# A decoder layer on one core: exponentials moved between ScalarE, VectorE and GpSimd

## The reference, cut to what matters

```python
# recurrence, for each feature, k = block input, v = ctx, ed = exp(-w), eg = exp(w)
out = A + jnp.exp(u + kk) * (vv * Bm + jnp.maximum(t - 1.0, 0.0))
A = ed * A + inc * jnp.exp(kk) * vv
Bm = eg * Bm + inc * jnp.exp(-kk)
# gates
logits = jnp.einsum('bsh,eh->bse', x, Wg)
Sm = jnp.swapaxes(jax.nn.softmax(logits, axis=-1), 1, 2)
```

## Time and profile before

| | |
|---|---|
| median of 3 runs | 1078.71 us (1078.17 to 1080.0) |
| profiled execution | 1075.21 us, of which its span is 1073.5 us |
| PE busy | 961.7 us (90%) |
| DVE busy | 738.1 us (69%) |
| ACT busy | 695.5 us (65%) |
| POOL busy | 103.8 us (10%) |
| mean granted clock of TensorE | 0.961 |

### The profile page before, as it was taken

One profiled execution on the slowest core, in us unless ns is written; L12 is line 12 of the kernel. 1 busy time (PEld: TensorE's weight loads), 2 busy tenths in 40 slices (PEclk: granted clock), 3 DMA queues, 4 the chain that ended last, 5 costly groups with the idle time before them and its releaser, 6 DMA issues.

```text
span 1073.5 us, 19089 instructions
## 1 busy us (share of the span) xinstructions
PE 961.7 (90%) x7280; PEld 868.4 (81%) x7280; DVE 738.1 (69%) x1476; ACT 695.5 (65%) x1231; POOL 103.8 (10%) x115
## 2 busy tenths in 40 slices
PE   6557788989799989999899989999899998999997
PEld 5457687778688878888798878988798887989997
DVE  6657758675687667776777748786667757555665
ACT  6347676666557766666676757566676666756775
POOL 2012001200130011200111001200012001000000
PEclk9669889999899999999999999999999999999999
DMA  6013233222122222222222222222222222232350
GB/s 197 28 53 97 81 108 116 62 59 70 60 80 70 70 70 88 59 80 83 75 81 77 64 87 79 60 80 60 79 80 79 60 70 77 82 118 89 101 186 11
DMA packets 89242, 86.49 MB, mean 81 GB/s; under 512 B 5944, under 2 KB 89152, under 8 KB 89152
## 3 DMA queue, kind: packets, MB, share of 16 engines
q1 hardware_dynamic: 89152, 85.27, 26.0%
HBM read 83.15 MB, written 2.10 MB: 79 GB/s over the span
## 4 chain that ended last, share of the span: by engine, by line
PE 70%; DVE 16%; ACT 10%; issue 3%; DMA 0%; POOL 0%; SPq 0%; POOLq 0%; ACTq 0%; DVEq 0%
PE up_ps L403 10%; PE up_ps L405 9%; PE up_ps L404 9%; PE down_ps L611 9%; PE down_ps L613 9%; PE down_ps L612 8%; DVE w_lo L786 4%; PE bank L403 3%; PE bank L404 3%; PE bank L405 3%; DVE h_lo L786 2%; ACT L670 2%; PE bank L454 2%; ACT w_hi L735 1%; ACT probs L670 1%
## 5 line engine op out<-in xcount | busy, mean ns | idle before, releaser
L724 ACT ACTIVATE h_all<-up_ps,b_all 128x512 f32<-128x512 f32 (+1 forms) x296 | 182.2, 630 | 299.1 <-PE up_ps L405 297.1
L611 PE MATMUL down_ps<-w_hi,h_hi 128*128 128x256 f32 x1024 | 297.9, 291 | 40.5 <-DVE h_lo L786 40.5
L786 DVE TENSOR_TENSOR w_lo<-w_raw,w_hi 128x512 fp32r<-128x512 f32 x296 | 206.8, 712 | 165.2 <-ACT w_hi L735 164.9
L613 PE MATMUL down_ps<-w_hi,h_lo 128*128 128x256 f32 x1024 | 291.8, 285 | 0.0
L612 PE MATMUL down_ps<-w_lo,h_hi 128*128 128x256 f32 x1024 | 291.7, 285 | 0.0
L611 PEld LDWEIGHTS down_ps<-w_hi,h_hi 128*128 128x128 f32 x1024 | 197.6, 193 | 52.0 <-DVE w_lo L786 39.6
L403 PE MATMUL up_ps<-x2t_hi,w_hi 128*128 128x512 f32 (+1 forms) x592 | 224.3, 379 | 0.0
L404 PE MATMUL up_ps<-x2t_lo,w_hi 128*128 128x512 f32 (+1 forms) x592 | 218.8, 370 | 0.0
L405 PE MATMUL up_ps<-x2t_hi,w_lo 128*128 128x512 f32 (+1 forms) x592 | 218.6, 369 | 0.0
L612 PEld LDWEIGHTS down_ps<-w_lo,h_hi 128*128 128x128 f32 x1024 | 197.9, 193 | 5.1
L613 PEld LDWEIGHTS down_ps<-w_hi,h_lo 128*128 128x128 f32 x1024 | 197.8, 193 | 0.0
(11 more groups left out here) (174 smaller groups left out, 1347.4 us busy)
## 6 DMA issues: line engine op xcount, KB each, us to landing
w_raw<-in_w_dram SPq DMA_DIRECT2D x296, 256.0 KB, 2.8
x_in<-in_x_dram SPq DMA_DIRECT2D x8, 256.0 KB, 3.2
ctx_sb<-in_ctx_dram SPq DMA_DIRECT2D x8, 256.0 KB, 3.1
out_dram<-acc SPq DMA_DIRECT2D x8, 256.0 KB, 3.2
w_raw<-in_wq_dram SPq DMA_DIRECT2D x1, 256.0 KB, 3.0
w_raw<-in_wk_dram SPq DMA_DIRECT2D x1, 256.0 KB, 4.1
w_raw<-in_wv_dram SPq DMA_DIRECT2D x1, 256.0 KB, 4.2
w_raw<-in_wo_dram SPq DMA_DIRECT2D x1, 256.0 KB, 4.6
```

Of the source, the lines that this page charges most:

```text
L611: nc.tensor.matmul(ps, hi, w2h[:, c, :], start=c == 0 and j == 0, stop=False, skip_group_check=True)
L613: mm = nc.tensor.matmul(ps, lo, w2h[:, c, :], start=False, stop=c == FC - 1 and j == PAIR - 1, skip_group_check=True)
L724: a = nc.scalar.activation(h_all[:, unit % HALL, k * wide:(k + 1) * wide], up_ps[unit % 2][:, k * wide:(k + 1) * wide], ACT.Gelu_apprx_tan ...
L786: return nc.vector.tensor_tensor(dst, src, hi.bitcast(F32), ALU.subtract)
```

## The change

The two `exp_uk` instructions on ACT are gone. A small tile `exp_u` = exp(u) is computed once in the setup, and the product on DVE becomes, in two halves, (`mix` * `exp_u`) * `exp_k`. Since `exp_k` is now needed there, `mix` lies in the tile `exp_uk`. The routing exponential goes from ACT to POOL, as e to the power of `logits`, with a constant tile `euler` full of e. In POOL's list it stands at step 62 of the pair's train.

```diff
-        mix = exp_k[:]
+        mix = exp_uk[:]
...
                     nc.scalar.activation(exp_k[:], k, ACT.Exp)
-                    for c in range(C):
-                        nc.scalar.activation(exp_uk[:, c], k[:, c], ACT.Exp, bias=wu[:, 1, c:c + 1])
...
-                if part == 3:
-                    act.wait_ge(route_step, 4 * b + 2)
-                    nc.scalar.activation(route_exps[:], logits[:], ACT.Exp).then_inc(route_exp, 1)
...
                 if s == V_STEP:
+                    nc.scalar.activation(exp_u[:], wu[:, 1, :], ACT.Exp)
...
                     dve.wait_ge(xa_step, 6 * p + 5)
-                    nc.vector.tensor_tensor(mix, mix, exp_uk[:], ALU.mult).then_inc(xa_step, 1)
+                    for c in range(C):
+                        i = nc.vector.scalar_tensor_tensor(out=mix[:, c], in0=mix[:, c], scalar=exp_u[:, c:c + 1], in1=exp_k[:, c],
+                                                           op0=ALU.mult, op1=ALU.mult)
+                    i.then_inc(xa_step, 1)
...
+            def route(b):
+
+                pool.wait_ge(route_step, 4 * b + 2)
+                nc.gpsimd.tensor_tensor(route_exps[:], euler[:], logits[:], ALU.pow).then_inc(route_exp, 1)
...
+            nc.gpsimd.memset(euler[:], math.e)
...
             for s in FIRST_ORDER[1:]:
                 attend(0, s)
+                if s == ROUTE_STEP[3]:
+                    route(0)
...
                         if p < NPAIR:
                             attend(p, s)
+                            if s == ROUTE_STEP[3]:
+                                route(p)
```

More of the change, by code:

```diff
@@ L3 @@
 import itertools
+import math
 from contextlib import ExitStack
@@ L100, in decoder_layer @@
         decay = sb("decay", [P, 2, C])
+        exp_u = sb("exp_u", [P, C])
         decay_row = sb("decay_row", [P, 2, C, S])
@@ L110, in decoder_layer @@
         eps_row = sb("eps_row", [P, PAIR])
+        euler = sb("euler", [P, PAIR, E])
         x_in = sb("x_in", [P, PAIR, D])
```

## The result

| | before | after |
|---|---|---|
| median of 5 runs each | 1078.71 us (1075.67 to 1080.0) | 1086.67 us (1084.75 to 1087.7) |
| profiled execution (its span) | 1075.21 us (1073.5) | 1087.0 us (1085.3) |
| mean granted clock in it | 0.961 | 0.956 |

The ratio is 1.0073, with a 95% interval of 1.0060 to 1.0086: the change makes the kernel slower by 8.0 us in the medians. The two profiled executions lie 11.8 us apart, because the one of before is among its fastest.

The account below looks back on a forecast made before the run. TensorE, busy 90%, was taken to bound the kernel. Terms -5.0 - 1.1 + 1.6 - 0.5 + 12.1 = +7.1 us on the profiled 1075.21, carried over to the median (3.5 more), gave 1085.8 us; range 1075 to 1098.

Parts of the forecast that it names:

- The power, X: Length of the 16-column routing power on GpSimd, taken as 2.5 us; the total moves up to 8 us per us.
- Both ends of the range: Bounds for the power: 0.8 us if its extra cost is paid once, 4.3 us if all is per column.
- the even split: Half of the power's extra 0.51 us taken as fixed and half per column, giving 2.5 us.
- What is waited for: DVE's route_sum waits for the power, delaying gates and h_lo and so PE in every pair: +12.1 us.
- the prediction's list: PE delays from the power: pair 0 2.3, pair 1 1.3, pairs 2, 4, 6 4.5, pairs 3, 5 3.3, pair 7 0.7 us.
- the port conflict: In pairs 3 and 5, x_bo on GpSimd beside DVE's gates and w_lo adds 0.3 and 0.7 us, 1.0 each.
- the hidden part: Part of DVE's delay not reaching PE: 1.47 us in pairs 3, 5, 7; 0.64 in 2, 4, 6; 1.1 in pair 1.
- The recurrence part: Dropping exp_uk saves 0.71 us in each of pairs 1 to 7, -5.0; the two-part DVE product costs 0.2 each, +1.6.
- The -0.5 of pair 1: x_bo leaves its place beside an h_lo in pair 1, gaining 0.5 us.
- Table loads: 14 loads around the routing exponential, 18.0 us of ACT, buy nothing; rival that they were on the path, 1054 us, chance 0.05.
- The clock: PE's large wait falls from 3.46 to 2.75 us, avoiding one clock fall of four, -1.1 us.
- The sum: All terms together: +7.1 us against the profiled execution of 1075.21 us.

Follow-up runs that it names:

- r1_recur_only: Changed kernel with the routing exponential back on ACT, so the recurrence part alone; 1072.45 us against 1077.76 for the kernel before, ratio 0.9945.
- r3: Kernel before with a copy in place of the routing exponential on ACT, which removes its 14 table loads; 1079.36 us, ratio 1.0008 to the kernel before.
- r11: Changed kernel with gates issued late, x_bo ahead of the power, ACT's exponential burst at step 45 and scans in two steps; 1071.21 us, ratio 0.9938.
- r5_power_twice: Changed kernel with the power computed twice in a row, the first result unread; 1113.51 us, ratio 1.0329 to the kernel before.
- r6_gates_late: Changed kernel with DVE's sum, reciprocal and gates issued two items later and PE's gate transposes one step later; 1079.73 us, ratio 1.0016.
- r4_power_8: Changed kernel with the power over 8 of the 16 columns; 1076.25 us, ratio 0.9978 to the kernel before.
- r8_bias_first: Changed kernel with x_bo of the next pair put ahead of the power in GpSimd's list; 1084.39 us, ratio 1.0059 to the kernel before.

## Why the prediction was right, and where two errors met

Forecast 1085.8, measured 1086.67, and the direction and the mechanism hold. Step by step:

- *The power, X.* Taken as 2.5, measured 2.90. With the run over 8 columns there are three points, 0.70, 1.64 and 2.90 us for 2, 8 and 16 columns: 0.157 for a column and 0.38 fixed. Both ends of the range were wrong and the even split was nearly right.
- *What is waited for.* The large new waits are where the text put them; it did not have the small ones at the gates of pairs 3 to 7 (0.28 to 0.40). By the prediction's list X = 2.90 would have cost 12.1 + 8 x 0.4 = 15.3; the new waits of pairs 0 to 7 in the trace add up to 2.34 + 1.34 + 1.23 + 1.11 + 1.55 + 1.11 + 1.56 + 0.88 = 11.1. In pairs 3 and 5 the port conflict took 0.12 and 0.54, 0.66 and not 1.0. Part of the rest is no saving, because a wait costs PE more than its idle time. Ahead of the wait of pair 4 the last up product counts as busy to its end, 0.39 us, while in the kernel before the `down` starts 0.23 behind it, and the first `down` behind a wait takes 0.36 instead of 0.28. With some 2.5 us of this kind (see the clock, below) the routing cost about 13.6, so the hidden part was sized too small by some 0.2 us a pair. The timeline of PE, before and then after:

```profile
548.45 0.39 PE L405 MATMUL up_ps<-x2t_hi,w_lo 128*128 128x512 f32 x1
548.68 0.28 PE L611 MATMUL down_ps<-w_hi,h_hi 128*128 128x256 f32 x1
...
555.42 0.39 PE L408 MATMUL up_ps<-x2t_hi,w_lo 128*128 128x512 f32 x1
557.08 0.36 PE L614 MATMUL down_ps<-w_hi,h_hi 128*128 128x256 f32 x1 [1.27 <-DVE h_lo L785]
```

- *The recurrence part.* 0.74 a pair, as taken (0.71). Alone it gave -5.9 by the ratio and -3.5 between the profiled executions, for -3.6 forecast in its expectation. The product costs 0.48 x 2, with `acc` as a good stand-in: PE's wait at the transposes grew by 0.19 or 0.20 us in every pair but pair 1, for 0.2 forecast.
- *The -0.5 of pair 1.* Not shown. Its waits at the transposes of the recurrence's result and of its normalization went from 3.32 + 1.94 to 4.24 + 0.29 (timeline of PE, before and then after), but in r1_recur_only, where `x_bo` stays in its place, they fell further, to 3.17 and nothing.

```profile
171.18 0.66 PE L532 MATMUL bank<-ident,exp_k 128*128 128x128 f32 x4 [3.32 <-DVE exp_k L912]
178.09 0.66 PE L540 MATMUL bank<-ident,x 128*128 128x128 f32 x4 [1.94 <-DVE x L804]
...
171.95 1.11 PE L535 MATMUL bank<-ident,exp_uk 128*128 128x128 f32 x4 [4.24 <-DVE exp_uk L914]
179.31 0.66 PE L543 MATMUL bank<-ident,x 128*128 128x128 f32 x4 [0.29 <-DVE x L803]
```

- *Table loads.* Worth nothing that can be measured: shown by r3, and r11 agrees. The Trainium skill, "ScalarE: Activation LUTs", section on what the load costs, puts a switch at 2.66 us with a drain. The rows have 1.28 for every load, and an ACTIVATE that waits for nothing else starts 0.01 us behind it; the measurement decides.
- *The clock. This step failed.* I counted one fall fewer because the large wait would be shorter, -1.1. Added up without the stretch at the very end, TensorE's granted clock was 1.2 GHz for 81.9 us in the profiled execution before and for 92.2 after. The wait of 2.72 came with a lower clock in all five pairs; that of 3.46 had done so in four. Of the other changes the clearest are new stretches at 74 us (behind the gates of pair 0) and at 245. PE's busy time rose by 5.1 us. Added up product by product over both traces, 2.9 of it lie in products that ran at the lower clock in one of the two, and 2.5 beside waits that only one of them has, as in the rows of pair 4 above; the rest is -0.3. So the clock cost 2.9 where the sum has -1.1. Over all runs the kernels differ less: the mean granted clock is 0.954 in the median of the changed kernel and 0.957 in that of the 51 runs of the kernel before that stand beside the experiments. The window behind the wait of pair 4, beside the second of the earlier trace rows, where the clock was 1.00 before; the granted clock is the third number from the end:

```profile
522.00:524.00 2.00, 2.00 (x10) 2.00 (x10) 0.31 (x2) 0.58 (x1) 0.00 (x0) 0.50 0.76 227
```

- *The sum against the profile.* The profiled executions differ by 11.8, not 7.1. PE's idle time accounts for 6.7 of it: +11.1 for the routing, -5.2 for the large waits, +1.4 for the product in seven pairs, -0.7 for the two waits of pair 1, +0.5 for the waits that follow the large ones in pairs 3 to 7 (they moved both ways, by -1.2 to +1.5), and -0.4 elsewhere. Its busy time is the other 5.1.
- *The two errors.* The sum was 4.7 too small. Against that, the 3.5 us by which the profiled execution of before lay under its median were carried over, but the one of after lies 0.3 above its median: 3.8 too much. The runs of the kernel before scatter over 1075 to 1081, and with them its clock: those over 1079 us have a mean granted clock of 0.949 or 0.950, nearly all of those under 1077 have 0.957 to 0.962. The profiled one is a low one. So it is luck that the forecast met the median to 0.9 us, while direction, order of size and place of the waits are not. That a sum from a profiled execution was carried over to a median was a source of error that I had not put into the range.

## What to carry to other kernels

Read the order of the instructions on the engine that waits before you move work off a busy engine: 18 us less on ACT bought nothing, while 2.9 us of latency in front of DVE's in-order list cost 11 us of waits in eight places, because part of it was hidden in each; the next 2.9 us, in r5_power_twice, cost their whole length eight times over. An operation on GpSimd that has only been seen on two columns needs a second size before it is used on sixteen. Where an engine's burst stands in front of a small copy that the bound engine needs, move the copy ahead of it, but expect the wait to move to the next item of the list and follow it there: three such steps took 1072.5 to 1059.6 us, though each time most or all of the wait came up again further on.

## What the runs showed of the hardware that I had not expected

A power on GpSimd costs 0.157 us for each column of 128 partitions, some 50 times an addition's (1.66 us for 512 columns, L1084, is 0.003). And a GpSimd instruction does not hold DVE off for its whole length in every case: `x_bo` did (a pair of `w_lo` went from 1.29 to 1.83 us), but a `w_lo` that began inside the power was not held: two of them passed in 1.30 us, and the power took 0.38 longer itself. The Trainium skill, "SBUF — State Buffer", section on the two separate sides, has the first to start keep the port pair for the whole instruction. The `x_bo` rows agree. The power's agree only with the first `w_lo`, which began ahead of it; by that rule the second would have waited for the end of the power, some 2.8 us on. A wait of 2.72 us came with a stretch at 1.2 GHz in 5 of 5 pairs in the profiled execution of the changed kernel and of r6_gates_late, in 4 of 5 of r4_power_8 and in 3 of 5 of r1_recur_only and r8_bias_first, with the same work around it; the stretch began between 0.8 us before the end of the wait and 1.6 us after it. One kernel's runs differ too, from 0.949 to 0.962 in the mean granted clock of the kernel before, so a single profiled execution does not tell two kernels apart in this; what decides it stays open.
